# Mixture-of-experts block loop: rows transposed in f32 with the rounding constant still in them, and TensorE's expert numbers read from one packed word

## The reference

```python
def activation_quant(x):
    scale = 127.0 / jnp.maximum(jnp.max(jnp.abs(x), axis=-1, keepdims=True), EPS)
    return jnp.clip(jnp.round(x * scale), -128.0, 127.0) / scale

def bitlinear(x, w):                      # weight_quant: weights to -1, 0, 1 times their mean
    return activation_quant(x) @ weight_quant(w).T

def expert_ffn(x, gw, uw, dw):
    gate = bitlinear(x, gw)
    up = bitlinear(x, uw)
    activated = up * jnp.square(jax.nn.relu(gate))
    return bitlinear(activated, dw)

top_w, top_i = jax.lax.top_k(softmax(x @ router_w.T), 2)      # 8 experts, 2 of them for a token
out = sum over e of combine[:, e] * expert_ffn(x, gate_w[e], up_w[e], down_w[e])   # 256 -> 512 -> 256
```

## Time and profile before

| | us |
|---|---|
| median of 3 runs | 536.68 (534.36 to 538.36) |
| profiled execution, its own time | 536.89 |
| its span, first to last instruction | 534.4 |
| PE busy, share of the span | 388.1 (73%) |
| DVE busy | 380.0 (71%) |
| ACT busy | 226.3 (42%) |
| mean granted TensorE clock | 0.860 |

### The profile page before, as it was taken

The page is one execution under the profiler, slowest core; times in us unless marked ns, Lnnn a source line. Parts: engine busy times, 40 slices in busy tenths (PEclk is TensorE's granted clock), DMA queues, the critical chain, the costliest instruction groups (busy, mean ns, idle before and its releaser), DMA issues.

```text
span 534.4 us, 11144 instructions
## 1 busy us (share of the span) xinstructions
PE 388.1 (73%) x3684; PEld 264.9 (50%) x3691; DVE 380.0 (71%) x927; ACT 226.3 (42%) x473; POOL 129.3 (24%) x135
## 2 busy tenths in 40 slices
PE   2557776752466667620999999999999999818892
PEld 1335654552233333310655756657557488716671
DVE  5998999867598898839749577595685737772451
ACT  2676888640267787720311231321313231224440
POOL 1091000000535553310000000095000059242332
PEclk9977788855577887955899999999999999958997
DMA  8944560221111222143321403402000170432000
GB/s 311 423 183 170 184 237 38 59 101 41 30 39 52 60 58 51 39 128 112 118 74 65 140 9 130 137 0 78 0 0 1 60 277 1 152 87 87 21 32 20
DMA packets 18133, 50.82 MB, mean 95 GB/s; under 512 B 2248, under 2 KB 6480, under 8 KB 17072
## 3 DMA queue, kind: packets, MB, share of 16 engines
q1 hardware_dynamic: 15152, 42.46, 22.0%
q0 software_dynamic: 2944, 7.88, 5.4%
HBM read 43.51 MB, written 6.82 MB: 94 GB/s over the span
## 4 chain that ended last, share of the span: by engine, by line
PE 51%; DVE 34%; issue 7%; DMA 3%; ACT 2%; POOL 1%; DVEq 1%; SPq 0%; ACTq 0%; POOLq 0%
PE bank L862 13%; PE bank L1080 7%; PE bank L970 5%; PE bank L871 5%; DVE mx L1368 4%; DVE hid L1534 3%; DVE hs L1536 3%; DVE hid L1533 3%; PE bank L882 2%; DVE raw L1407 2%; PE bank L906 2%; PE bank L782 2%; PE bank L929 2%; PE bank L916 2%; PE bank L756 2%
## 5 line engine op out<-in xcount | busy, mean ns | idle before, releaser
L566 POOL TENSOR_TENSOR WE<-WE,wT 128x512 f32<-128x512 f32 x32 | 40.4, 1301 | 181.0 <-DMA WE<-_L_ffn_expert_masks_dram 181.0
L1580 DVE TENSOR_TENSOR roped<-bank,cst 128x512 f32<-128x512 f32 x96 | 61.8, 685 | 30.7 <-PE bank L862 29.5
L546 POOL DMA_INDIRECT xg<-x_rows,owner_b x24 | 23.6, 983 | 117.1 <-DVE owner_b L391 94.8
L862 PE MATMUL bank<-XNT_hi,AW_hi 128*128 128x512 f32 x96 | 41.6, 433 | 0.5
L1233 ACT ACTIVATE prob<-prob 128x512 f32<-128x512 f32 x16 | 10.0, 631 | 69.2 <-DVE prob L1589 69.2
L862 PE MATMUL bank<-XNT_hi,AW_lo 128*128 128x512 f32 x96 | 37.9, 394 | 0.0
L862 PE MATMUL bank<-XNT_lo,AW_hi 128*128 128x512 f32 x96 | 37.8, 393 | 0.0
L756 PE MATMUL bank<-W,xgT 128*128 x90 | 30.3, 466 | 2.7 <-ACT xgT L1175 1.1
L871 PE MATMUL bank<-roped,MW 128*64 128x512 f32 x128 | 31.0, 605 | 0.0
L970 PE MATMUL bank<-VW,ctxT 128*128 128x256 f32 x128 | 30.8, 386 | 0.0
L553 POOL DMA_INDIRECT y_rows<-y,slot x24 | 23.7, 986 | 26.6 <-ACT y L1194 23.5
(11 more groups left out here) (290 smaller groups left out, 978.1 us busy)
## 6 DMA issues: line engine op xcount, KB each, us to landing
raw<-in_L_ffn_w_dram SPq DMA_DIRECT2D x8, 1536.0 KB, 6.8
f_all<-in_L_xattn_fold_dram SPq DMA_DIRECT2D x8, 768.0 KB, 4.4
kv<-in_keys_values_dram SPq DMA_DIRECT2D x8, 656.0 KB, 7.8
WE<-_L_ffn_expert_masks_dram SPq DMA_DIRECT2D x5, 768.0 KB, 6.6
WE<-_L_ffn_expert_masks_dram SPq DMA_DIRECT2D x3, 1024.0 KB, 9.1
f_rot<-in_L_xattn_rot_dram SPq DMA_DIRECT2D x8, 256.0 KB, 5.1
yg<-y_rows SPq DMA_DIRECT2D x8, 256.0 KB, 4.7
x_tok<-pay SPq DMA_DIRECT2D x8, 256.0 KB, 2.2
```

What stands on the lines that cost most here:

```text
L546: pool.indirect_dma_start(out=xg[j % 4][:].bitcast(U32), out_offset=None, in_=x_rows, in_offset=bass.IndirectOffsetOnAxis(ap=RB.owner[:, j ...
L566: pool.tensor_tensor(WE[:, e], WE[:, e], wT[:], ALU.mult).then_inc(WE_ready, 1)
L862: mm = pe.matmul(bank[g][:], a[:, k, c * P:(c + 1) * P], b[:, k, g * 512:(g + 1) * 512], start=k == 0 and i == 0, stop=k == 1 and i == 2)
L1580: ins = dve.tensor_tensor(roped[n][:, r, :].rearrange("p (b s) -> p b s", s=S), src, cst[:, None, at:at + S].to_broadcast([P, 8, S]), ALU. ...
```

## The change

- `integers` and `hid_q` are gone. PE transposes `hid` itself, in f32 and with MAGIC still added, against the f32 identity, and waits for ACT's `hidden_scaled` in place of DVE. MAGIC is subtracted by ACT in `hidden_rows`: Identity with the bias `less_magic` (-MAGIC for each partition) from an f32 bank of PSUM, in place of a Copy from bf16.
- `hidden` on DVE waits for turn_hidden(j-4) (`h_turned`) before it writes over `hid`. Its wait for the reciprocal stands behind the scale h[5], which doesn't need it.
- DVE packs, before the loop, the experts of seven blocks in a row (3 bits each) into one word for each of five starting blocks 0, 4, 8, 12, 16 (`run_e`), in six small instructions. PE loads one such word at the head of each iteration and gets each expert number by a shift and a mask. Before, it loaded two numbers from `block_ei` for each block.
- In the fourth stage the copy of `owner_d` moves ahead of two small DVE instructions.

```diff
@@ -21,6 +21,7 @@
 NE = 8
 FF = 512
 NBLK = 24
+RUN = 7
 XROW = 258
 QMAX = 127.0
 NE_D = 32
...
@@ -159,6 +161,8 @@
         below = sb("below", [P, NBLK, NE])
         block_e = sb("block_e", [P, NBLK])
         block_ei = sb("block_ei", [P, NBLK], U32)
+        run_part = sb("run_part", [P, NBLK // 4 - 1])
+        run_e = sb("run_e", [P, NBLK // 4 - 1], U32)
         below2 = sb("below2", [P, NBLK, NE])
         block_w = sb("block_w", [P, 2, NBLK])
         w_prod = sb("w_prod", [P, 2, NE])
...
@@ -193,7 +197,6 @@
         xgT = [sb(f"xgT{i}", [P, H], BF16) for i in range(2)]
         relu = [sb(f"relu{i}", [P, FF]) for i in range(2)]
         hid = [sb(f"hid{i}", [P, FF]) for i in range(4)]
-        hid_q = [sb(f"hid_q{i}", [P, FF], BF16) for i in range(2)]
         hidT = [sb(f"hidT{i}", [P, FF], BF16) for i in range(2)]
         y = [sb(f"y{i}", [P, H]) for i in range(2)]
...
@@ -748,6 +751,13 @@
             def expert_of(j):
                 return pe.value_load(block_ei[0:1, bass.ds(j, 1)], min_val=0, max_val=NE - 1)
 
+
+            def run_of(i):
+                return pe.value_load(run_e[0:1, bass.ds(i, 1)], min_val=0, max_val=(1 << 3 * RUN) - 1)
+
+            def in_run(word, k):
+                return (word >> (3 * k)) & (NE - 1)
+
             def gate_up(j, par, e):
                 pe.wait_ge(xgT_ready, j + 2)
                 pe.wait_ge(hid_done, j + 1)
@@ -757,11 +767,11 @@
                                        W[:, bass.ds(e, 1), m, k * FF:(k + 1) * FF].rearrange("p a i -> p (a i)"), start=k == 0, stop=k == 1)
                 mm.then_inc(gu_ready, 1)
 
-            def turn_hidden(j, par):
-                pe.wait_ge(hq_ready, j + 1)
-                pe.wait_ge(hT_ready, j + 1)
+
+            def turn_hidden(j, r):
+                pe.wait_ge(hid_scaled, j + 1)
                 for k in range(4):
-                    mm = pe.transpose(bank[5].bitcast(BF16)[:, k * P:(k + 1) * P], hid_q[par][:, k * P:(k + 1) * P], ident[:])
+                    mm = pe.transpose(bank[5][:, k * P:(k + 1) * P], hid[r][:, k * P:(k + 1) * P], identf[:])
                 mm.then_inc(h_turned, 1)
 
             def down(j, par, e):
@@ -806,19 +816,22 @@
                 turn_rows(j, 0, j)
                 if j:
                     gate_up(j - 1, (j - 1) % 2, expert_of(j - 1))
+            pe.wait_ge(runs_ready, 1)
             with pe.Fori(0, NBLK // 4 - 1) as i:
+                word = run_of(i)
                 for r in range(4):
                     j = 4 * i + r
-                    e_up, e_down = expert_of(j + 3), expert_of(j)
-                    turn_hidden(j, r % 2)
+                    e_up, e_down = in_run(word, r + 3), in_run(word, r)
+                    turn_hidden(j, r)
                     turn_rows(j + 4, i + 1, r)
                     gate_up(j + 3, (r + 1) % 2, e_up)
                     down(j, r % 2, e_down)
+            word, last = run_of(NBLK // 4 - 2), expert_of(NBLK - 1)
             for j in range(NBLK - 4, NBLK):
-                e_down = expert_of(j)
-                turn_hidden(j, j % 2)
+                e_down = in_run(word, j - NBLK + 8) if j < NBLK - 1 else last
+                turn_hidden(j, j % 4)
                 if j + 3 < NBLK:
-                    gate_up(j + 3, (j + 1) % 2, expert_of(j + 3))
+                    gate_up(j + 3, (j + 1) % 2, last)
                 down(j, j % 2, e_down)
                 if j == NBLK - 4:
                     fold_queries(0, 0, 0, A_BANKS_0)
@@ -1185,7 +1198,7 @@
 
             def hidden_rows(j, par):
                 act.wait_ge(h_turned, j + 3)
-                act.activation(hidT[par][:], bank[5].bitcast(BF16)[:, 0:FF], ACT.Copy).then_inc(hT_ready, 1)
+                act.activation(hidT[par][:], bank[5][:], ACT.Identity, bias=less_magic[:]).then_inc(hT_ready, 1)
 
             def outputs(j, h, par, r):
@@ -1332,6 +1345,7 @@
         @block.vector
         def _(dve):
             link = Chain(dve, dve_chain)
+            dve.memset(less_magic[:], -MAGIC)
             dve.memset(magic[:], MAGIC).then_inc(magic_set, 1)
             dve.memset(bank[6][:], 0.0).then_inc(a_cleared, 1)
 
@@ -1520,6 +1534,12 @@
                 link(dve.tensor_tensor(below2[:], below[:], w_prod[:, k:k + 1, :].to_broadcast([P, NBLK, NE]), ALU.mult))
                 link(dve.tensor_reduce(block_w[:, k, :], below2[:], AX.X, ALU.add))
             dve.sem_inc(block_w_ready, 1)
+            seventh = 4 * (NBLK // 4 - 2) + 1
+            so_far = block_e[:, RUN - 1:RUN - 1 + seventh:4]
+            for k in range(RUN - 2, 0, -1):
+                link(dve.scalar_tensor_tensor(run_part[:], so_far, float(NE), block_e[:, k:k + seventh:4], ALU.mult, ALU.add))
+                so_far = run_part[:]
+            dve.scalar_tensor_tensor(run_e[:], so_far, float(NE), block_e[:, 0:seventh:4], ALU.mult, ALU.add).then_inc(runs_ready, 1)
 
 
             dve.sem_inc(hid_done, 2)
@@ -1528,33 +1548,25 @@
 
                 par, h = r % 2, hs[r]
                 if not isinstance(j, int) or j >= 4:
-                    dve.wait_ge(hq_ready, j - 3)
+                    dve.wait_ge(h_turned, j - 1)
                 dve.wait_ge(relu_ready, j + 1)
                 link(dve.scalar_tensor_tensor(hid[r][:], bank[1 + par][:], 0.0, relu[par][:], ALU.max, ALU.mult))
                 dve.tensor_tensor(hid[r][:], hid[r][:], bank[3 + par][:], ALU.mult).then_inc(hid_done, 1)
                 dve.wait_ge(hid_done, j + 3)
                 link(dve.tensor_reduce(h[:, 1:2], hid[r][:], AX.X, ALU.max, apply_absolute_value=True))
                 link(dve.tensor_scalar(h[:, 2:3], h[:, 1:2], h[:, 0:1], EPS, ALU.mult, ALU.max))
-                link(dve.reciprocal(h[:, 3:4], h[:, 2:3]))
+                inverse = dve.reciprocal(h[:, 3:4], h[:, 2:3])
                 dve.tensor_scalar(h[:, 5:6], h[:, 2:3], block_w[:, 1, bass.ds(j, 1)], None, ALU.mult)
+                link(inverse)
                 dve.tensor_scalar(h[:, 4:5], h[:, 3:4], h[:, 0:1], QMAX, ALU.mult, ALU.mult).then_inc(h_scale_ready, 1)
-
-            def integers(j, par, r):
-                dve.wait_ge(hid_scaled, j + 1)
-                dve.wait_ge(h_turned, j + 1)
-                dve.tensor_scalar(hid_q[par][:], hid[r][:], MAGIC, None, ALU.subtract).then_inc(hq_ready, 1)
 
             for j in range(4):
                 hidden(j, j)
-                if j:
-                    integers(j - 1, (j - 1) % 2, j - 1)
             with dve.Fori(1, NBLK // 4) as i:
                 link.enter(i - 1, 16)
                 for r in range(4):
                     hidden(4 * i + r, r)
-                    integers(4 * i + r - 1, (r - 1) % 2, (r - 1) % 4)
                 link.leave(NBLK // 4 - 1, 16)
-            integers(NBLK - 1, (NBLK - 1) % 2, (NBLK - 1) % 4)
 
 
             dve.sem_inc(roped_ready, 2)
@@ -1717,10 +1729,10 @@
             ends = end[:, None, :].to_broadcast([P, NT, NE_D])
             link(dve.tensor_tensor(picked_d[:], ends, cst[:, C_TILE:C_TILE + NT, None].to_broadcast([P, NT, NE_D]), ALU.is_le))
             link(dve.tensor_reduce(first_e[:], picked_d[:], AX.X, ALU.add))
+            dve.wait_ge(one_hots_summed, 1)
+            dve.tensor_copy(owner_d[:], bank[2][:, 0:NT]).then_inc(owner_d_ready, 1)
             link(dve.tensor_tensor(turns_at[:], first_e[:], cst[:, C_IOTA:C_IOTA + NT], ALU.add))
             link(dve.tensor_scalar(final_at[:], turns_at[:, 1:NT], 4.0, None, ALU.add))
-            dve.wait_ge(one_hots_summed, 1)
-            dve.tensor_copy(owner_d[:], bank[2][:, 0:NT]).then_inc(owner_d_ready, 1)
             n = 8 * NGROUP
             link(dve.tensor_tensor(at_pair[:], cst[:, C_IOTA:C_IOTA + n, None].to_broadcast([P, n, NT - 1]),
                                    turns_at[:, None, 1:NT].to_broadcast([P, n, NT - 1]), ALU.is_ge))
```

More of the change, by code:

```diff
@@ L152, in build @@
         magic = sb("magic", [P, 1])
+        less_magic = sb("less_magic", [P, 1])
         w_rec = [sb(f"w_rec{i}", [P, 3]) for i in range(2)]
@@ L320, in build @@
         h_scale_ready, relu_ready = sem("h_scale_ready"), sem("relu_ready")
-        hid_done, hq_ready, h_turned, hT_ready, y_ready, y_copied = (sem(n) for n in ("hid_done", "hq_ready", "h_turned", "hT_ready", "y_ready", "y_copied"))
+        hid_done, runs_ready, h_turned, hT_ready, y_ready, y_copied = (sem(n) for n in ("hid_done", "runs_ready", "h_turned", "hT_ready", "y_ready", "y_copied"))
         y_stored = [sem(f"y_stored{i}") for i in range(2)]
```

## The result

The changed kernel took 533.94 us (median of 15 runs, 530.99 to 546.54) beside 536.68 us (median of 15) of the kernel before: a ratio of 0.995, 95% interval 0.9925 to 0.9974. That is a gain of 2.7 us where 10.3 were forecast, outside the forecast range of 522 to 533 us and within 1% of no change. A few executions ran over 1.5% above the fastest of their kernel; they are counted among the runs and left out of the ratios. The profiled execution took 532.38 us, 1.6 us under the median, and has a span of 530.0 us, 4.4 us less than before.

What follows compares the result with a forecast made beforehand. DVE was taken to bound the first experts' block loop, PE close behind. Rounds 64.9 + boundaries 1.5 + waits 1.7 = 68.1 us against 77.8; with -0.4 and -0.4, -10.5 in all: 526.4 us, range 522.3 to 533.

Steps and rivals of the forecast that it cites:

- What else: Remaining terms: the loop's 1.7 us of waits kept, packing free, loop's end -0.4 us, owner_d's copy -0.4 us.
- Rival 2: ACT and PE take over: every round loses 0.2 to 0.3 us to waits, 531 us; chance 0.20.
- PE's loop end: Branch and one word load at PE's loop boundary, priced at 0.3 us for DVE, five times: 1.5 us.
- DVE's round: One block on DVE in the first experts' loop: from 3.31 us to 2.82, between 2.78 and 3.08.
- (a): L1545 goes from DVE's round; the next block's first instruction follows L1540 at 0.15 us, where L1545 led it by 0.33.
- (b): L1539 no longer waits for the reciprocal on DVE: reciprocal to L1540 goes from 0.45 to 0.26 us.
- Rival 1: The clock stays up: low stretches in the loop vanish and the 1.7 us of waits go, 524.7 us; chance 0.17.
- ACT's floor: ACT's round: 2.82 us busy a block, real floor near 2.65 through overlapping instructions, just under DVE.
- Rivals 3 and 4: No effect, rounds stay at 3.3 us, 535 us, chance 0.08; f32 transposes at low clock, 548 us, chance 0.05.
- The loop's end: After the last block: PE's 0.7 us load moves ahead, less dearer transposes and copies, plus 0.2 from the reciprocal: -0.4 us.
- owner_d: Fourth stage: its copy moves ahead of two DVE instructions, so POOL's first gather starts earlier: -0.4 us.
- Outside the loop: Terms beyond the block loop's rounds: -0.4 us at its end and -0.4 us for owner_d's copy.

Runs made afterwards that it cites:

- experiment 1: Half of the change each, against the kernel before: packed words alone 535.05 us; all else, with the two expert-number loads a block kept, 537.46 us.
- word_only: The kernel before with the packed words alone; bf16 transposes, L1545 and the old order of the reciprocal stay: 535.05 us, ratio 0.9975, on chip 8.
- bf16_third: The changed kernel with rows turned in bf16, rounding to integers left out, measured on chip 11: 535.12 us, ratio 0.9941.
- unrolled_fifth: The changed kernel with PE's loop written out, measured on chip 14: 530.5 us, ratio 0.9875.
- bf16_turn: The changed kernel with rows turned in bf16, rounding to integers left out, measured on chip 8: 528.78 us, ratio 0.984.
- pe_unrolled: The changed kernel with PE's five loop iterations written out, measured on chip 8: 525.55 us, ratio 0.979.
- clock_kept: The changed kernel with unused matmuls added, one a block and four at each iteration's end on PE: 524.78 us on chip 0, 525.71 on chip 15.

## Why the prediction was wrong, by its own steps

The step that failed is in "What else": "The waits of 1.7 us that the loop has now over its floor I keep". In the first measurement there were 9.3 us over a floor of 2.79 us a round, in place of 1.7. About 3 of them stand in the four rounds in which a post came late; 3.5 in two rounds at 4.5 us, at PE's loop ends with the clock down to 0.50 to 0.57, both behind such a stop; 2.1 at DVE's loop ends, the rest at PE's other ones and in the last round. No row of the profile before shows a late post, and the prediction had no rival for one. The same error is in the range: its upper end of 533 us rests on the low clock, not on a wait for PE that ends after PE's work. Rival 2 (ACT and PE take over, 531 us) named the right waiters, ACT for PE, but for another reason and in all rounds; 17 of the 23 rounds are within 0.2 us of the floor or of a loop end's length. Its sign was met all the same: DVE waited 6.8 us for relu in the 23 rounds, 0.30 us a block where the sign was 0.1, but nearly all of it in the rounds named here.

On chips 0 and 15 the forecast of 526.4 us came true (526.87 and 527.04), and the loop too (68.3 and 68.1 us, forecast 68.1). That is in part luck: the sum missed DVE's loop ends (2.1 us), and it had 0.7 too much for DVE's rounds, 0.9 for PE's loop ends and about 0.2 in the waits that it kept. The terms one by one:

- **DVE's round** 2.82 forecast, 2.79 measured; (a) 0.15 was 0.12, (b) 0.26 was 0.20 to 0.26. Right.
- **DVE's loop end** was missing from the sum. The prediction read the step to the next block inside the loop alone. A round across it is 0.47 to 0.52 us longer, four times, 2.1 us with the loop's entry (0.14); L1545 had hidden 0.3 of each.
- **PE's loop end** was priced at 0.3 us five times, 1.5 us. It cost DVE 0.15 four times, 0.6 us, at full clock.
- **The low clock** (in the 1.7 us kept): 1.0 to 1.3 us in one round, which took 4.39 us on chip 0 and 4.08 on chip 15, and 3.07 and 3.04 with the clock kept up. Right in size. Rival 1's condition, a clock of 1.00 through the loop, came about only with matmuls added: then the kernel takes 524.8 us on chip 0 and 525.7 on chip 15, where rival 1 had 524.7.
- **ACT's floor** of 2.65 us took the overlap off twice: busy time by stretch counts overlapping instructions once already. With 2.72 + 0.10 = 2.82 ACT stood level with DVE, not under it; measured on chip 0 it is busy 2.76 us a block beside DVE's 2.79. The forecast had less room here than it said. **ACT's hidT** 680 ns, forecast 695. **PE's f32 transposes** 0.60 us at full clock, as in the earlier trace rows. **Both halves are needed**: right, by experiment 1. Rivals 3 and 4 did not come.
- **The loop's end** had -0.4 us from the last product to the last y. It was +0.2 (8.28 before, 8.51 after): the load of 0.7 us is gone, but the last blocks are set by the chain of ACT and PE, not by DVE's last product, and from y of block 20 on it is 8.34 us against 8.98. The 0.6 us is there, but behind DVE's last product, where the sum counted it, it does not show.
- **owner_d**: POOL's gather follows the copy at 0.96 us before and after. The two instructions that stood ahead of the copy, 0.40 us from 472.35 to 472.75, are behind it now, so copy and gather stand 0.4 us earlier behind what comes before them, as forecast. That the kernel ends earlier by it is not shown: from the gather to the end of the span it is 60.7 us before and 60.9 in word_only, which has the old order, and 60.8 after, 61.1 on chip 0 and 60.4 on chip 15.
- **Outside the loop** the sum had -0.8 us. The span without the loop is 456.6 us before and 456.5 after, 456.7 on chip 0 and 454.4 on chip 15: no run shows the 0.8, and profiles differ by more than that.

What the late posts are is not settled. Three things are shown.

First, all kernels profiled in one measurement agree: with late posts on chips 11 and 14 and in the first, without on chips 0, 8, 13 and 15, and the changed kernel's times do not overlap (524.9 to 528.7 us and 529.9 us or more). As no chip was measured twice, it can be the chip or something else of that measurement.

Second, late posts need neither f32 transposes (bf16_third), nor PE's loop or the low clock (unrolled_fifth). The kernel before has none in its one profile, which is from the first measurement, and takes 536.5 to 537.8 us on every chip. That the short rounds bring them is likely but not shown: the packed words are in every kernel that had them too, and word_only ran on chip 8 alone.

Third, where they come, the trace itself lacks events: it holds 3684 semaphore events in the first measurement and 3660, 3662, 3671 and 3614 in the four other profiles with late posts, but 4151 in the kernel before and 4115 to 4141 in the fourteen other profiles without. Of the 16 posts of block 0's scatter at 155.7 us two are there; on chip 0 all 16. Most of those missing are posts of DMA queues in the loop, 376 in the first measurement against 613 on chip 0; from 140 to 236 us 15 of PE's 102 and 18 of ACT's 125 are missing too. Whether the events and PE's posts are held up by one cause, and whether recording the events is part of it, was not tried.

The Trainium skill, "NOTIFIC — the notification-queue block", section "3. Interfaces", has it that the block which takes such records can stall an engine when one of its internal FIFOs fills. Missing events would fit a block that is full; no run here shows the block, or that it stalled PE.

The Trainium skill, "Perfetto Trace Analysis", section "Per-instruction lifecycle: what the profiler-reported window actually captures", says that a matmul's end is estimated and that its semaphore is pushed only once PSUM has acknowledged the writes. The trace fits: 157.80 by the record and 159.24 by the post. Whether the writes themselves were late or only the post, it does not tell; by the record alone PE looks idle and ACT at fault.

## What to carry to other kernels

A long instruction ahead of a loop end can hide most of what the loop end costs, on DVE here 0.3 us of 0.46. Whoever takes it away should read the step across the loop end too, not only the one inside, and consider writing out both loops: here that is the fastest kernel, 522.4 to 523.5 us on three chips without late posts, 13.5 to 14.2 us below the kernel before. Where two engines are nearly level, clear both in the same edit: of the loop's 9.5 us one half alone gave 1.3 and the other lost 0.8. When a result contradicts a sum whose short rounds read as forecast in the profile, measure the unaltered kernel again, on another chip, before blaming a part of it: bf16_turn and pe_unrolled, each alone, would have given a wrong culprit.

## What the hardware showed that was not expected

- PE's semaphore posts can come up to 1.4 to 2.2 us behind the end of the matmul's record (first measurement), two to four of them within 0.2 us. They do so in all five profiles of chips 11, 14 and the first measurement, and in none of the fourteen of chips 0, 8, 13 and 15. It costs 5 us of a 67 us loop with PE's loop written out, and 5 to 7 us in the changed kernel (73.4 to 74.9 us against 68.1 and 68.3).
- A loop end on DVE costs 0.46 us behind an instruction of 0.20 us and 0.16 us behind one of 0.42 us. At PE's loop ends the array stood 5.3 us for issue in all, in the first measurement (the row of L774) and on chip 0, but that cost DVE only 0.15 us a time at full clock.
- On chip 0 PE was busy 1.88 us of the 4 from 206 on, at a loop end, and the granted clock fell to 0.67 from 210 to 214 us; on chip 15 it fell to 0.64 from 162 to 166 us. With clock_kept's unused matmuls in the holes it is 1.00 from 206 to 214 us. The medians are 2.1 and 1.3 us lower with them, though the runs of chip 15 overlap (524.9 to 528.7 and 524.7 to 526.1 us). A loop end is not needed for a fall: with PE's loop written out the clock is 0.72 from 206 to 210 us on chip 8, behind 4 us in which PE was busy 2.30.
